# A routed feed-forward layer whose gate/up weights are the stationary operand and are fetched per tile

## The reference

```
probs = softmax(x @ gate_w.T);  w, idx = top_k(probs, 2);  w = w / sum(w)
for each of 8 experts (gup: 1024x128, dn: 128x512, ce: the token's weight for this expert or 0):
    g, u = split(x @ gup.T, 2)            # 512 and 512 values per token
    acc += ce * ((silu(g) * u) @ dn.T)
```

## Time and profile before

| what | value |
|---|---|
| median of 3 runs | 651.42 us (649.82 to 651.47) |
| span of the profiled execution | 649.3 us |
| TensorE busy, matmuls | 592.1 us, 91% |
| TensorE busy, weight loads (beside matmuls) | 383.1 us, 59% |
| VectorE busy | 462.0 us, 71% |
| ScalarE busy | 413.9 us, 64% |
| GpSimd busy | 110.2 us, 17% |
| DMA, mean over the span | 45 GB/s |

### The profile page before, as it was taken

One profiled execution on the slowest core, in us unless ns is written; L12 is line 12 of the kernel. 1 busy time (PEld: TensorE's weight loads), 2 busy tenths in 40 slices (PEclk: granted clock), 3 DMA queues, 4 the chain that ended last, 5 costly groups with the idle time before them and its releaser, 6 DMA issues.

```text
span 649.3 us, 10805 instructions
## 1 busy us (share of the span) xinstructions
PE 592.1 (91%) x3516; PEld 383.1 (59%) x3516; DVE 462.0 (71%) x1396; ACT 413.9 (64%) x807; POOL 110.2 (17%) x118
## 2 busy tenths in 40 slices
PE   3579997879999999999989999699999999999995
PEld 1162252326556464655555766466768887888885
DVE  3746756644486637887958889978659996996744
ACT  2108998968688988689979554354564356445541
POOL 1000002320011422100362103511013111001200
PEclk9587999989999999999999999899999999999999
DMA  8931000120001130000130001400010000000000
GB/s 273 407 152 38 2 1 0 55 77 10 5 18 55 37 89 21 14 14 13 39 108 9 17 18 41 109 17 14 21 27 25 2 17 2 1 0 18 1 18 18
DMA packets 28183, 29.26 MB, mean 45 GB/s; under 512 B 4953, under 2 KB 24289, under 8 KB 27745
## 3 DMA queue, kind: packets, MB, share of 16 engines
q1 hardware_dynamic: 26080, 24.36, 11.3%
q0 software_dynamic: 2048, 4.20, 2.3%
HBM read 19.51 MB, written 9.04 MB: 44 GB/s over the span
## 4 chain that ended last, share of the span: by engine, by line
PE 68%; issue 6%; ACT 3%; DVE 3%; POOL 1%; DMA 1%; POOLq 0%; SPq 0%; DVEq 0%; ACTq 0%
PE bank L887 16%; PE bank L903 8%; PE bank L805 8%; PE bank L1044 7%; PE bank L894 4%; PE bank L984 2%; PE bank L961 2%; PE bank L776 2%; PE bank L699 2%; PE bank L700 2%; PE bank L701 2%; PE bank L879 1%; PE bank L977 1%; POOL x_rows L1754 1%; PE bank L858 1%
## 5 line engine op out<-in xcount | busy, mean ns | idle before, releaser
L1122 ACT ACTIVATE a_big<-feat,txt_cols 128x512 f32<-128x512 f32 x270 | 173.7, 713 | 4.6 <-PE bank L805 4.3
L887 PE MATMUL bank<-gup_sb,x_cols 128*128 x240 | 126.5, 614 | 0.5 <-ACT x_cols L1163 0.4
L805 PE MATMUL bank<-a_big,score_pad 128*32 128x512 f32 x616 | 102.7, 614 | 3.2 <-ACT a_big L1122 3.1
L1237 ACT ACTIVATE a_big<-bank,cols_sb 128x512 f32<-128x512 f32 x72 | 49.2, 687 | 56.7 <-PE bank L701 55.8
L903 PEld LDWEIGHTS bank<-down_sb,hid_sb 128*128 128x128 f32 x480 | 62.3, 191 | 31.9 <-issue 31.9
L1527 DVE SCALAR_TENSOR_TENSOR gated_sb<-gated_sb,bank 128x256 f32<-128x256 f32 x120 | 50.0, 417 | 42.4 <-ACT gated_sb L1188 41.7
L1044 PEld LDWEIGHTS bank<-rw_sb,a_big 128*128 128x128 f32 x576 | 69.4, 192 | 2.8
L1044 PE MATMUL bank<-rw_sb,a_big 128*128 128x128 f32 x576 | 69.9, 275 | 0.0
L903 PE MATMUL bank<-down_sb,hid_sb 128*128 x480 | 64.0, 276 | 2.7 <-ACT hid_sb L1170 2.6
L1188 ACT ACTIVATE gated_sb<-bank 128x256 f32<-128x256 f32 x120 | 45.8, 382 | 30.8 <-PE bank L887 30.0
L1529 DVE SCALAR_TENSOR_TENSOR gated_sb<-gated_sb,bank 128x256 f32<-128x256 f32 x120 | 50.5, 421 | 4.1
(11 more groups left out here) (279 smaller groups left out, 952.4 us busy)
## 6 DMA issues: line engine op xcount, KB each, us to landing
gup_sb<-gup SPq DMA_DIRECT2D x1, 4096.0 KB, 15.7
y_rows<-x_tiles SPq DMA_DIRECT2D x60, 64.0 KB, 1.5
down_sb<-down SPq DMA_DIRECT2D x1, 2048.0 KB, 17.4
x_rows<-b_y SPq DMA_DIRECT2D x2, 960.0 KB, 10.4
x_tiles<-x_rows SPq DMA_DIRECT2D x4, 448.0 KB
rw_sb<-rw SPq DMA_DIRECT2D x1, 1152.0 KB, 19.7
a_qT<-x_T SPq DMA_DIRECT2D x4, 256.0 KB, 2.7
a_tok<-x_tok SPq DMA_DIRECT2D x4, 256.0 KB, 3.0
```

Source lines behind the costliest of these rows:

```text
L805: last = mm(P[2][32 * j:32 * j + 32, :], score_pad[:, 31 - i:63 - i], ring[k % RING], start=(i == 0), stop=(KCOL * (i + 1) + j >= KEYS))
L887: mm(P[3 + h][:, :], x_col[i % 2], part[:, bass.ds(at_of[i], I0)], start=True, stop=True)\
L1122: act(ring[(k + j) % RING], feat[b][:, :], ACT.Tanh, bias=txt_cols[:, c:c + 1])\
L1237: act(hid6[u % 2][:, c * S:(c + 1) * S], P[5 + n % 2][:, :], ACT.Gelu, bias=col("rb1", n))\
```

## The change

`mix_up` makes the weights the stationary operand: eight products per tile (four per half), each with a 128 by 128 block of the expert's weights held still and the 128 columns of transposed rows moving. What comes out is features by tokens. The gated values are thus already in the form in which `mix_down` needs them, `turn_h`, ScalarE's copy and `hid_sb` are gone, and `mix_down` stands in the step n = 2i + 3 behind that step's `mix_up`. `gup_sb` becomes three buffers of one tile's weights each, 512 KB. SP reads the tile's expert into a register and fetches its weights from DRAM (128 partitions by two runs of 2 KB): tiles 0 and 1 of a batch in the step n = -1, tile m + 2 in the step n = 2m, once TensorE has done the up products of the tile that had the buffer before (three tiles earlier). The store of tile m - 2 stands behind that fetch in SP's order. The 4 MB load at the start is gone. ScalarE's tanh waits for the down projection of the tile two before instead of its transposes.

```diff
--- before.py
+++ after.py
@@ -40,6 +40,7 @@
 I1 = 256
 C1 = I1 // 128
 TOPK = 32
+GUPS = 3
 ROUNDS = TOPK // 8
 BIG = 3.0e38
 NEG = 1.0e30
@@ -262,7 +263,7 @@
         score_pad = sb("score_pad", 63)
         two = sb("two", 2 * T)
         neg_half = sb("neg_half", T)
-        gup_sb = sb("gup_sb", E * 2 * I0)
+        gup_sb = [sb(f"gup_sb{k}", 2 * I0) for k in range(GUPS)]
         down_sb = sb("down_sb", E * I0)
         rw1_hi = sb("rw1_hi", (E + 1) * I1, F32R)
         rw1_lo = sb("rw1_lo", (E + 1) * I1, F32R)
@@ -296,7 +297,6 @@
         x_tiles = sb("x_tiles", NT * 128)
         x_cols = sb("x_cols", 2 * 128)
         gated_sb = sb("gated_sb", 2 * S)
-        hid_sb = sb("hid_sb", 2 * S)
         picked_sb = sb("picked_sb", 2 * T * 128)
         rho_e_sb = sb("rho_e_sb", T * KP)
         rho_m_sb = sb("rho_m_sb", T * KP)
@@ -413,7 +413,6 @@
         picked = [span(picked_sb, k * 128, 128) for k in range(2 * T)]
         x_col = [span(x_cols, k * 128, 128) for k in range(2)]
         gated = [span(gated_sb, k * S, S) for k in range(2)]
-        hid_T = [span(hid_sb, k * S, S) for k in range(2)]
         hid6 = [span(a_big, k * C1 * S, C1 * S) for k in range(2)]
 
         s_toh = a_s[:, :].rearrange("p (t o h) -> p t o h", o=SLOTS, h=HEADS)
@@ -515,6 +514,7 @@
         share_step = sem("share_step")
         share_ready = sem("share_ready")
         scattered = sem("scattered")
+        gup_in = [sem(f"gup_in{k}") for k in range(GUPS)]
         rows_loaded = [sem(f"rows_loaded{g}") for g in range(len(X_GROUPS))]
         xT_psum = sem("xT_psum")
         xT_ready = sem("xT_ready")
@@ -522,8 +522,6 @@
         gate_tanh = sem("gate_tanh")
         gate_half = sem("gate_half")
         gated_ready = sem("gated_ready")
-        hT_psum = sem("hT_psum")
-        hT_ready = sem("hT_ready")
         y_psum = sem("y_psum")
         y_ready = sem("y_ready")
         y_stored = [sem(f"y_stored{k}") for k in range(4)]
@@ -645,7 +643,22 @@
 
             def gate_tile(b, n):
 
+                def expert(i):
+
+                    at = eng.value_load(offsets[b][0:1, i:i + 1], min_val=0, max_val=(E - 1) * I0)
+                    k = NT * b + i
+                    if k >= GUPS:
+                        eng.wait_ge(gu_psum, 2 * (k - GUPS + 1))
+                    eng.dma_start(gup_sb[k % GUPS][:, :].rearrange("p (h f) -> p h f", h=2),
+                                  gup[:, :, bass.ds(at, I0)]).then_inc(gup_in[k % GUPS], 16)
+
+                if n == -1:
+                    eng.wait_ge(offsets_ready, b + 1)
+                    for i in range(GUPS - 1):
+                        expert(i)
                 i = n // 2 - 2
+                if n % 2 == 0 and i + 1 + GUPS < NT:
+                    expert(i + 1 + GUPS)
                 if n % 2 == 0 and i >= 0:
                     if i == 0 and b >= 1:
                         for t in range(T):
@@ -679,7 +692,6 @@
             for k in range(2):
                 eng.dma_start(x_rows[k].rearrange("(i p) f -> p i f", p=128),
                               b_ys[0][:, 0:128].unsqueeze(1).broadcast_to([128, NT, 128])).then_inc(rows_clear, 16)
-            eng.dma_start(gup_sb[:, :], gup).then_inc(tail_weights_in, 16)
             eng.dma_start(down_sb[:, :], down).then_inc(tail_weights_in, 16)
             eng.dma_start(rw2_sb[:, :], rw2).then_inc(tail_weights_in, 16)
             steps = {"load_a": load_a, "load_ctx": load_ctx, "load_rows": load_rows, "gate": gate_tile, "store": store,
@@ -872,41 +884,34 @@
                     for g, (first, end) in enumerate(X_GROUPS):
                         if i == first:
                             eng.wait_ge(rows_loaded[g], 16 * (b + 1))
-                    if done + max(i - 2, 0) >= 1:
-                        eng.wait_ge(hT_ready, done + max(i - 2, 0))
-                    if i >= 1:
+                    if done + i >= 1:
                         eng.wait_ge(xT_ready, done + i)
                     eng.transpose(P[5][:, 0:128], tile_rows[i], ident).then_inc(xT_psum, 1)
 
                 def mix_up(i, h):
                     if h == 0:
                         eng.wait_ge(xT_ready, done + i + 1)
+                        eng.wait_ge(gup_in[(done + i) % GUPS], 16 * ((done + i) // GUPS + 1))
                     if i >= 1:
                         eng.wait_ge(gated_ready, 2 * (done + i - 1) + h + 1)
-                    part = gup_sb[:, h * E * I0:(h + 1) * E * I0]
-                    mm(P[3 + h][:, :], x_col[i % 2], part[:, bass.ds(at_of[i], I0)], start=True, stop=True)\
-                        .then_inc(gu_psum, 1)
-
-                def turn_h(i):
+                    for c in range(C0):
+                        w = tile(gup_sb[(done + i) % GUPS], C0 * h + c)
+                        last = mm(tile(P[3 + h], c), w, x_col[i % 2], start=True, stop=True)
+                    last.then_inc(gu_psum, 1)
+
+                def mix_down(i):
                     eng.wait_ge(gated_ready, 2 * (done + i + 1))
-                    eng.wait_ge(xT_ready, done + min(i + 3, NT))
-                    for c in range(C0):
-                        last = eng.transpose(tile(P[5], c), tile(gated[i % 2], c), ident)
-                    last.then_inc(hT_psum, 1)
-
-                def mix_down(i):
-                    eng.wait_ge(hT_ready, done + i + 1)
                     if done + i >= 1:
                         eng.wait_ge(y_ready, done + i)
                     for c in range(C0):
                         w = down_sb[:, c * 128:][:, bass.ds(at_of[i], 128)]
-                        last = mm(tile(P[7], i % 4), tile(hid_T[i % 2], c), w, start=(c == 0), stop=(c == C0 - 1))
+                        last = mm(tile(P[7], i % 4), tile(gated[i % 2], c), w, start=(c == 0), stop=(c == C0 - 1))
                     last.then_inc(y_psum, 1)
 
                 if n == -1:
                     eng.wait_ge(offsets_ready, b + 1)
                     if b == 0:
-                        eng.wait_ge(tail_weights_in, 48)
+                        eng.wait_ge(tail_weights_in, 32)
                         eng.wait_ge(fp_ready, 2)
                     expert(0)
                     turn_x(0)
@@ -914,12 +919,10 @@
                 if h == 0 and i + 1 < NT:
                     expert(i + 1)
                     turn_x(i + 1)
-                if h == 1 and 1 <= i <= NT:
-                    turn_h(i - 1)
                 if i < NT:
                     mix_up(i, h)
-                if h == 0 and 2 <= i <= NT + 1:
-                    mix_down(i - 2)
+                if h == 1 and 1 <= i <= NT:
+                    mix_down(i - 1)
 
 
             def keys(b):
@@ -1162,13 +1165,6 @@
                         eng.wait_ge(gu_psum, 2 * (done + i - 1))
                     act(x_col[i % 2], P[5][:, 0:128], ACT.Copy).then_inc(xT_ready, 1)
 
-                def turned_h(i):
-
-                    eng.wait_ge(hT_psum, done + i + 1)
-                    if i >= 2:
-                        eng.wait_ge(y_psum, done + i - 1)
-                    act(hid_T[i % 2], P[5][:, :], ACT.Copy).then_inc(hT_ready, 1)
-
                 def take(i):
 
                     eng.wait_ge(y_psum, done + i + 1)
@@ -1179,12 +1175,10 @@
                     return
                 if h == 0 and i + 1 < NT:
                     turned_x(i + 1)
-                if h == 1 and 1 <= i <= NT:
-                    turned_h(i - 1)
                 if i < NT:
                     eng.wait_ge(gu_psum, 2 * done + n + 1)
                     if i >= 2:
-                        eng.wait_ge(hT_psum, done + i - 1)
+                        eng.wait_ge(y_psum, done + i - 1)
                     act(gated[i % 2][:, h * 256:(h + 1) * 256], P[3 + h][:, 0:256], ACT.Tanh, scale=0.5)\
                         .then_inc(gate_tanh, 1)
                 if h == 0 and 2 <= i <= NT + 1:
@@ -1830,7 +1824,7 @@
         "gate": f(n["L0_ffn_gate_w"].T),
         "router": f(n["L1_ffn_router_w"]),
         "rb2": f(n["L1_ffn_rb2"]),
-        "gup": f(gup.transpose(2, 0, 1).reshape(D, E, 2, 2, I0 // 2).transpose(0, 3, 1, 2, 4).reshape(D, E * 2 * I0)),
+        "gup": f(gup.transpose(2, 0, 1).reshape(D, E, 2, 2, I0 // 2).transpose(0, 3, 1, 2, 4).reshape(D, 2, E * I0)),
         "down": f(down.reshape(E, D, C0, 128).transpose(3, 0, 2, 1).reshape(128, E * I0)),
         "rw1": f(rw1.transpose(1, 0, 2).reshape(D, (E + 1) * I1)),
         "rw2": f(rw2.reshape(E + 1, C1, 128, D).transpose(2, 0, 1, 3).reshape(128, (E + 1) * I1)),
```

## The result

The changed kernel takes 660.07 us (655.45 to 661.08, 4 runs), the kernel before 651.01 us (649.82 to 651.47, 4 runs). The ratio is 1.0123, 95% interval 1.0086 to 1.0160, which is about 8 us slower; the medians are 9.1 apart. 638.5 was forecast, with 626 to 650 as the range. The profiled execution has a span of 658.9 us, 9.6 more than before. The change's own runs follow TensorE's granted clock: the one of 655.45 us had 0.962 in the mean, the three of 659.43 to 661.08 had 0.950 to 0.953.

A forecast was written before the change was run, and what follows sets the result against it. TensorE's own program was taken to set the pace. From the 649.3 us span, -22.8 - 2.6 + 10 + 2.5 = -12.9 gave 636.4, or 638.5 us by the runs' measure; range 626 to 650.

The forecast's parts named there:

- The steady cost of the new products: Gate/up products on TensorE: sixteen records in 1.78 us instead of 1.72 per tile, +3.6 us over 60 tiles.
- rival with loads in series: Gate/up products: weight loads not hidden, twelve more per tile at 0.19 us, some 770 us in all; chance 0.02.
- The fetches in the middle of a batch: Weights fetched per tile in steady state: fetch 5.2 us at most, cover 6.1 us, so nothing on the path.
- The starts: First up product of each batch: late by 4.7, 1.1, 0 and 5.1 us waiting for weights; +10 us taken.
- The 1.2 GHz stretch after the pause was there before; it moves and does not grow: TensorE's low clock behind the pauses at the starts of batches: same length as before, no added time.
- -22.8: TensorE, all tiles: -26.4 us for transposes of gated values removed, +3.6 us for the turned gate/up products.
- VectorE's lack of room: Batch 2: VectorE at 94% once TensorE has less work; bounds 0 and 5 us, +2.5 us taken.
- the growing wait for gated values: A sign named beforehand that the prediction is wrong: TensorE waiting longer for gated values; no size given.
- another engine takes the pace: Rival: half of the 22.8 us saved on TensorE turns into waits for gated values, 647 us; chance 0.14.
- The copy of y: Up product's wait for ScalarE's copy of the previous tile's y: down ends half a step earlier, so costed at nothing.
- the 2.6 us of waits for `hid_sb`: Down projections at ends of batches: waits in three places for the copy of transposed gated values go, -2.6 us.
- The rival that was slower by late fetches: Three buffers too few, each tile's fetch late: 0.9 us per tile over 30 dense tiles, 664 us; chance 0.11.

The follow-up runs named there:

- e2_one_expert: The changed kernel without fetches: the 4 MB loaded once at the start, every tile using expert 0's weights; 643.19 us, ratio 0.987 to the kernel before.
- e1_early: The changed kernel with the fetches of each batch's first three tiles ahead of the loads of the sorted rows in SP's order; 655.07 us.
- e8_ahead_two: The changed kernel with a batch's first two fetches in the previous batch's last steps (batch 0: ahead of row loads), the third behind row loads; 644.83 us.

## Why the prediction was wrong, point by point

*The steady cost of the new products: right.* Sixteen records of up take 1.79 us on the chain, 1.78 was taken from the last layer's down projection. Over all tiles they cost some 4.3 us more than the old ones at their steady pace, by the table below, where 3.6 was forecast. Weight loads are hidden: sixteen of 0.19 us in series would be 3.0 us. The rival with loads in series, and the Trainium skill's rule in "TensorE: Matmul & The Clock Gate", "What overlaps and what doesn't", by which it was made, are not borne out by this trace.

*The fetches in the middle of a batch: right.* 512 KB land in 4.0 us (3.9 estimated), and no tile but the first ones waits.

```profile
gup_sb<-gup SPq DMA_DIRECT2D x60, 512.0 KB, 4.0
```

*The starts: right in kind, and the waits nearly right in size.* 4.7, 1.1, 0 and 5.1 were forecast, and TensorE waited 3.9, 0.5, 1.7 and 5.1, 11.3 in all, where the sum had 10. The queue served in order, as assumed. In batch 2 the forecast had compared the landing with the old time of the first up product, but TensorE now came to it 2 us sooner after the issue of the row loads.

*"The 1.2 GHz stretch after the pause was there before; it moves and does not grow": wrong.* This was the first step to fail. At the start of batch 3 the clock was low from 416 to 432 instead of for some 3 us, and from 422.8 on it halved the pace of work on the path; in batch 0 it was low for 10 us instead of 3. Constants multiplied in the pauses gave 7.4 us back. In the kernel before they gave 2.0, so some 5 us are what the change added. The sum had 0 for this.

*"-22.8", the TensorE time saved: right as busy time, wrong as time gained.* This was the second step to fail, and the larger. I read a busy TensorE and a chain without gaps as room of the other engines, and put VectorE's lack of room at 2.5 us by its busy share, in one batch. What the busy share did not show was the loop: up product, tanh, two operations on VectorE, and the next up product in the same bank. The windows were to shrink by 5 to 6 us each and moved by -1.7, -2.3, +0.4 and +1.5; of the prediction's own signs of being wrong, the growing wait for gated values came true, 6.2 us in the trace after. How far it bound is seen from the distances between the starts of TensorE's records: whatever goes beyond the steady step of a shape (0.112 us for a record of 128 columns, 0.432 for 512) is a gap. From 139 us to the end of batch 3:

| | before | e2_one_expert |
|---|---|---|
| transposes of gated values, 240 by 0.109 | 26.2 | 0 |
| up products at their steady step | 102.5 | 106.8 |
| gaps ahead of up products | 6.4 | 16.7 |
| gaps ahead of the transposes | 2.4 | 0 |
| gaps ahead of down projections | 4.6 | 7.9 |
| gaps, all | 32.4 | 46.5 |

-26.2 + 4.3 + 14.1 is -7.8, and the spans differ by 7.9. So 14 of the 22 us saved turned into gaps; some 2 of them that the rows do not show stand ahead of the transposes of the next rows. A wait for gated values that `turn_h` used to make now stands ahead of the up product, with 0.44 us less work in front of it, and VectorE's other operations stand in the way. For example, ahead of the up record at 460.56 in batch 3, the addition behind the cross attention (L1601, from 457.08) and the normalisation behind it keep VectorE busy. So the tanh that was ready at 458.04 is taken up only at 459.63:

```profile
457.65 0.39 ACT L1182 ACTIVATE gated_sb<-bank 128x256 f32<-128x256 f32 x1 [1.23 <-PE bank L899]
```

```profile
457.08 1.12 DVE L1601 SCALAR_TENSOR_TENSOR b_y<-bank,rx_den,b_y 128x128 f32<-128x128 f32 x4
458.23 0.87 DVE L1255 BATCH_NORM_STATS2 b_stats<-b_y 128x6 f32<-128x128 f32 x4
459.14 0.38 DVE L1259 BATCH_NORM_AGGREGATE b_mv<-b_stats 128x2 f32<-128x6 f32 x4
459.55 0.17 DVE L1262 TENSOR_SCALAR b_var<-b_mv 128x4 f32<-128x4 f32 x1
459.63 0.42 DVE L1521 SCALAR_TENSOR_TENSOR gated_sb<-gated_sb,bank 128x256 f32<-128x256 f32 x1
```

```profile
460.56 1.16 PE L899 MATMUL bank<-x_cols,gup_sb 128*128 128x128 f32 x8 [1.04 <-DVE gated_sb L1523]
```

The rival "another engine takes the pace" had this mechanism, at half of the gain and a chance of 0.14; it took two thirds. Halving VectorE's part of the loop returned 5.7 of the 14 us, and nothing in the kernel before. The other 8 are open: gaps ahead of the down projection (for ScalarE's copy of y) and small ones ahead of many groups. Letting the down projection go ahead of that copy was not tried.

*The copy of y: costed at nothing, and wrong by about 3.* The wait of the down projection for it is 2.8 us in the trace after; the 2.6 us of waits for `hid_sb` that were to go came back under this name.

The miss of 21.6 us adds up from the parts. The products were to give -22.8 - 2.6 + 2.5 = -22.9 and gave -7.9 (e2_one_expert), 15 us short: that is the loop, with the copy of y in it. The rest of the change was to cost 10 and cost 17 (the change less e2_one_expert): 11.3 us of waits, and 5 to 6 that fit the clock. Both errors lie on the same side, so the range was missed by 10 us. The rival that was slower by late fetches named the right sign for a reason that did not occur: no tile in the middle of a batch waited.

## What to carry to other kernels

In this kernel, time taken from a busy engine was gained only as far as the loop that feeds it had slack. Measure that loop against the work between its ends, not the busy shares (in e2_one_expert 1.3 us from the end of an up product to its gated values at best, 1.8 in the median, over 4 in some tiles with other work in VectorE's order). A pause of TensorE of 3 us and more cost its length and then work behind it at half the clock; products of constants put into such a pause gave back 2.0, 3.3 and 7.4 us in three kernels. When data is fetched piece by piece, the pieces at the boundary of a loop need a place in the order of the iteration before, and ahead of a load that is awaited they only pass the wait on.

## What the runs showed of the hardware

TensorE's granted clock stayed at 0.50 for 16 us at the start of batch 3, through 9 us in which TensorE was busy for most of the time (3.41 and 3.82 of 4.00 us), while the kernel before had some 3 us of low clock in all at the same place. In the change, pauses of 3.5 and 0.6 us (rows awaited) and one of 5.1 us (weights awaited) stood one behind the other; in the kernel before, only 3.0 and 0.7 us. Transfers of one queue landed in the order of issue, and row loads issued behind 1.5 MB of weights kept TensorE waiting for up to 10.6 us (e1_early). A doubled memory traffic, some 27 MB more than before, left the windows of the batches unchanged (e8_ahead_two beside e2_one_expert).
